# Scan stage of a ViT tower: a three-part bf16 split moved from VectorE to TensorE and ScalarE, and new instruction orders

## The reference, cut to what matters

```python
xm   = silu(conv4(xn @ W_in.T)[..., :256]); z = (xn @ W_in.T)[..., 256:]
Bt   = xm @ W_B.T          # 16 numbers per token
Ct   = xm @ W_C.T          # 16 numbers per token
dt   = softplus(xm @ W_dt.T + b_dt)            # 256 per token
dA   = exp(-exp(log_A)[None, None] * dt[..., None])
dBx  = dt[..., None] * Bt[:, :, None, :] * xm[..., None]
h    = scan over tokens of h = dA * h + dBx    # 256 x 16 states
y    = (h * Ct[:, :, None, :]).sum(-1)
out  = residual + (y * silu(z)) @ W_out.T
```

## Time and profile before

| | |
|---|---|
| median of 3 runs | 2949.59 us (2949.24 to 2952.46) |
| the profiled execution's own time | 2955.88 us |
| its span in the profile | 2954.1 us |
| VectorE busy over the span | 2447.7 us, 83% |
| TensorE busy | 2455.6 us, 83% |
| GpSimd busy | 1978.0 us, 67% |
| ScalarE busy | 1511.1 us, 51% |
| granted TensorE clock, mean | 0.924 |

### The profile page before, as it was taken

How to read it: one execution, slowest core, us unless ns; L and a number is a source line. 1 busy time by engine, 2 the same in 40 slices (tenths; PEclk the granted TensorE clock), 3 DMA queues, 4 the chain that set the end, 5 groups by cost and what they waited for, 6 DMA issues and landing times. The chain is left out here.

```text
span 2954.1 us, 25221 instructions
## 1 busy us (share of the span) xinstructions
PE 2455.6 (83%) x6718; PEld 1146.3 (39%) x6718; DVE 2447.7 (83%) x3527; ACT 1511.1 (51%) x2542; POOL 1978.0 (67%) x1008
## 2 busy tenths in 40 slices
PE   6899898898998898988973068438999999998998
PEld 2344444444444444444431033213444444444443
DVE  4999999999999999999997822137888888888875
ACT  5666666666666666676652134234444433443332
POOL 3888888888888887888882068755555555555540
PEclk9999999999999999999996579758999999999999
DMA  2333323323333323324231024310000000000000
GB/s 83 110 94 98 109 92 105 106 87 117 94 99 107 100 91 108 103 87 119 89 102 51 0 50 71 36 51 22 29 29 29 29 29 29 29 29 29 26 22 11
DMA packets 169758, 199.27 MB, mean 67 GB/s; under 512 B 38969, under 2 KB 156946, under 8 KB 169490
## 3 DMA queue, kind: packets, MB, share of 16 engines
q1 hardware_dynamic: 158354, 189.27, 20.9%
q0 software_dynamic: 11264, 8.40, 2.2%
HBM read 164.37 MB, written 33.25 MB: 67 GB/s over the span
## 5 line engine op out<-in xcount | busy, mean ns | idle before, releaser
L905 POOL TENSOR_TENSOR a_hc<-a_h,a_cs 128x896 f32<-128x896 f32 (+1 forms) x448 | 891.6, 2002 | 182.1 <-DVE a_h L744 181.2
L360 PE MATMUL a_y_bank<-a_hc,a_ident 128*128 128x448 f32 (+1 forms) x1792 | 766.7, 562 | 14.7 <-POOL a_hc L905 13.6
L537 ACT ACTIVATE a_da<-a_dt,a_neg_a 128x448 f32<-128x448 f32 (+1 forms) x896 | 548.4, 632 | 331.3 <-DVE a_h L744 330.3
L744 DVE TENSOR_TENSOR_SCAN a_h<-a_da,a_h,a_dbx 128x448 f32<-128x448 f32 x528 | 583.1, 1134 | 14.2 <-ACT a_da L537 11.9
L360 PEld LDWEIGHTS a_y_bank<-a_hc,a_ident 128*128 128x128 f32 x1792 | 344.1, 196 | 359.9 <-issue 287.2
L2086 POOL TENSOR_TENSOR c_prod<-c_prob,c_qkv 128x1024 f32<-128x1024 f32 x100 | 280.7, 2849 | 274.6 <-DVE c_prob L1973 274.6
L1670 PE MATMUL c_p_ACC<-c_sc,c_w_ex 128*128 128x512 f32 x800 | 365.4, 594 | 0.0
L2079 POOL TENSOR_TENSOR c_prod<-c_qkv 128x1024 f32<-128x1024 f32 x100 | 231.9, 2341 | 152.7 <-ACT c_qkv L1754 152.7
L728 DVE TENSOR_TENSOR a_dbx<-a_dtx,a_b_bank 128x896 f32<-128x896 f32 (+1 forms) x308 | 328.5, 1067 | 4.5 <-PE a_b_bank L353 0.7
L1947 DVE TENSOR_TENSOR c_sc<-c_hid,c_p_CB 128x1024 f32<-128x1024 f32 x200 | 239.9, 1214 | 69.6 <-PE c_p_CB L1662 67.1
L893 POOL TENSOR_TENSOR a_dbp<-a_dtx,a_bs 128x896 f32<-128x896 f32 (+1 forms) x140 | 269.7, 1936 | 0.3
(11 more groups left out here) (297 smaller groups left out, 3688.3 us busy)
## 6 DMA issues: line engine op xcount, KB each, us to landing
a_cs<-c_rows SPq DMA_DIRECT2D x96, 896.0 KB, 5.3
a_bs<-c_rows SPq DMA_DIRECT2D x24, 1120.0 KB, 5.7
a_cs<-c_rows SPq DMA_DIRECT2D x16, 900.0 KB, 4.4
c_x<-h_rows SPq DMA_DIRECT2D x25, 256.0 KB, 2.8
heads<-c_ot SPq DMA_DIRECT2D x25, 256.0 KB, 2.3
c_dealt<-heads SPq DMA_DIRECT2D x200, 32.0 KB, 1.9
rolled<-c_res SPq DMA_DIRECT2D x25, 256.0 KB, 2.1
h_rows<-a_th SPq DMA_DIRECT2D x24, 224.0 KB
```

The lines of the kernel that those rows point to most:

```text
L360: pe.matmul(y_bank[:, d, 0:g.w], ident[:], hc[:, (g.i * NS + n) % HC_RING, d, 0:g.w], start=(n == 0), stop=(n == NS - 1)).then_inc(s_sum, 1)
L537: act.activation(da[:, k % DA_RING, 0:g.w], dt[g.slot][:, d, 0:g.w], ACT.Exp, scale=neg_a[:, d * NS + n:d * NS + n + 1]).then_inc(s_da, 1)
L744: dve.tensor_tensor_scan(h[:, n, d, 0:g.w], da[:, (g.i * 2 * NS + k) % DA_RING, 0:g.w], x, state, ALU.mult, ALU.add).then_inc(s_scan, 1)
L905: pool.tensor_tensor(hc[:, (q.i * NS + n) % HC_RING, :, 0:q.w], h[:, n, :, 0:q.w], cs[:, n % C_RING, 0:q.w].unsqueeze(1).to_broadcast([P, ...
```

## The change

B's split: ScalarE rounds the PSUM tile to bf16 as before. Then TensorE subtracts that rounded part from the PSUM tile itself: a bf16 matmul with a matrix `less` (minus the identity in the columns 64 to 127, zero elsewhere) accumulates into the bank that still holds the result. ScalarE copies the remainder as bf16 (partitions 64 to 127), a second such matmul subtracts it for partitions 96 to 127, and ScalarE copies the rest. The bank is given back after this last copy. `split_b` and `low_b` on VectorE are gone. `one_more` is now an Identity activation with bias 1 on ScalarE. VectorE makes the two `less` matrices at the start. `WORK_ORDER` moves the transposed output (`trh`) to bank 0 and `logit` to bank 1. The lists of calls of PE, ACT, DVE and POOL are written in a new order; SP's list is as before.

```diff
-              ("dt1", 0, 1), ("out", 0, -1), ("trh", 1, -1), ("cen2", 0, -1), ("var2", 1, -1), ("tok", 1, 2),
-              ("logit", 0, -1), ("cen", 0, 2), ("var", 1, 2), ("trn", 1, -1))
+              ("dt1", 0, 1), ("out", 0, -1), ("trh", 0, -1), ("cen2", 0, -1), ("var2", 1, -1), ("tok", 1, 2),
+              ("logit", 1, -1), ("cen", 0, 2), ("var", 1, 2), ("trn", 1, -1))
...
+            def less_high():
+                if p:
+                    pe.wait_ge(s_bch, p.i + 1)
+                    pe.matmul(tile_of("bc", p)[:, 0:p.w], less[:, 0, :], bc[p.slot][:, 0:p.w], start=False, stop=True,
+                              skip_group_check=True).then_inc(s_less, 1)
+
+            def less_middle():
+                if p:
+                    pe.wait_ge(s_bcm, p.i + 1)
+                    pe.matmul(tile_of("bc", p)[:, 0:p.w], less[:, 1, :], bc[p.slot][:, 0:p.w], start=False, stop=True,
+                              skip_group_check=True).then_inc(s_less, 1)
...
             def middle_b():
                 if p:
-                    taken(act, "bc", p)
-                    act.copy(bc[p.slot][64:128, 0:p.w], bcr[64:128, 0:p.w]).then_inc(s_bcm, 1)
+                    act.wait_ge(s_less, 2 * p.i + 1)
+                    act.copy(bc[p.slot][64:128, 0:p.w], tile_of("bc", p)[64:128, 0:p.w]).then_inc(s_bcm, 1)
+
+            def low_b():
+                if p:
+                    act.wait_ge(s_less, 2 * p.i + 2)
+                    act.copy(bc[p.slot][96:128, 0:p.w], tile_of("bc", p)[96:128, 0:p.w]
+                             ).then_inc(s_free[nth["bc", p.i][0]], 1)
+
+            def one_more():
+                if p:
+                    act.wait_ge(s_spe, p.i + 1)
+                    need(act, s_spm, p.i)
+                    act.activation(yt[:, :, 0:p.w], spe[:, :, 0:p.w], ACT.Identity, bias=1.0).then_inc(s_spu, 1)
...
+        dve.tensor_scalar(less[:, 0, 64:P], ident[:, 64:P], -1.0, None, ALU.mult)
+        dve.tensor_scalar(less[:, 1, 96:P], ident[:, 96:P], -1.0, None, ALU.mult)
+        dve.memset(less[:, 0, 0:64], 0.0)
+        dve.memset(less[:, 1, 0:96], 0.0)
...
-            def split_b():
-                if p:
-                    w = p.w
-                    dve.wait_ge(s_bch, p.i + 1)
-                    dve.tensor_tensor(bcr[64:128, 0:w], tile_of("bc", p)[64:128, 0:w], bc[p.slot][64:128, 0:w],
-                                      ALU.subtract).then_inc(s_free[nth["bc", p.i][0]], 1)
-
-            def low_b():
-                if p:
-                    w = p.w
-                    dve.wait_ge(s_bcm, p.i + 1)
-                    dve.tensor_tensor(bc[p.slot][96:128, 0:w], bcr[96:128, 0:w], bc[p.slot][96:128, 0:w],
-                                      ALU.subtract).then_inc(s_bc, 1)
-
-            def one_more():
-                if p:
-                    w = p.w
-                    dve.wait_ge(s_spe, p.i + 1)
-                    need(dve, s_spm, p.i)
-                    dve.tensor_scalar(yt[:, :, 0:w], spe[:, :, 0:w], 1.0, None, ALU.add).then_inc(s_spu, 1)
```

More of the change, by code:

```diff
@@ L1 @@
 from contextlib import ExitStack
+from dataclasses import dataclass
 import numpy as np
@@ L479, in tensor @@
             taps(0, 0)
+            taps(0, 1)
+            b_row(2)
+            taps(1, 0)
             last_sum(14)
             last_sum(15)
-            b_row(2)
-            taps(0, 1)
-            taps(1, 0)
             b_row(4)
+            taps(1, 1)
             sum_state(0)
-            taps(1, 1)
-            sum_state(1)
-            b_row(5)
             gate(0)
             gate(1)
+            b_row(5)
+            step(0)
             b_row(7)
-            step(0)
+            sum_state(1)
             b_and_c()
             b_row(8)
+            step(1)
             sum_state(2)
-            step(1)
+            out()
             sum_state(3)
-            out()
             b_row(10)
+            turn_out()
             sum_state(4)
             b_row(11)
+            less_high()
             sum_state(5)
-            turn_out()
             center_out()
+            less_middle()
+            sum_state(6)
+            variance_out()
+            sum_state(7)
             b_row(13)
-            sum_state(6)
-            sum_state(7)
-            variance_out()
+            token()
             sum_state(8)
-            token()
+            b_row(14)
             logit()
+            center()
             sum_state(9)
+            variance()
+            next_b_row()
             sum_state(10)
-            b_row(14)
-            center()
-            variance()
             sum_state(11)
+            turn_norm()
             sum_state(12)
-            turn_norm()
-            next_b_row()
             sum_state(13)
@@ L678, in scalar @@
             decays(5)
+            decays(6)
             biased(0)
-            decays(6)
-            keep_b_and_c()
             decays(7)
             biased(1)
-            middle_b()
+            decays(8)
             small_exp()
-            decays(8)
+            keep_b_and_c()
+            one_more()
             decays(9)
             keep_rows()
+            middle_b()
+            decays(10)
             square_out()
+            low_b()
+            decays(11)
+            log_of_sum()
             tail()
-            log_of_sum()
-            decays(10)
-            decays(11)
             scale_out()
@@ L835, in vector @@
             scans(1, 0)
+            product(2)
             scans(1, 1)
-            product(2)
-            gated()
             scans(2, 0)
@@ L841, in vector @@
             scans(3, 0)
+            gated()
             scans(3, 1)
@@ L846, in vector @@
             scans(4, 1)
+            scans(5, 0)
             product(7)
-            scans(5, 0)
             scans(5, 1)
@@ L851, in vector @@
             scans(6, 1)
-            split_b()
+            scans(7, 0)
             product(8)
-            scans(7, 0)
             scans(7, 1)
@@ L857, in vector @@
             scans(8, 0)
+            scans(8, 1)
             product(10)
-            scans(8, 1)
             scans(9, 0)
+            scans(9, 1)
             product(11)
[L862 to L865, removed]
             scans(10, 0)
@@ L868, in vector @@
             scans(11, 0)
-            normed_out()
+            lost()
             scans(11, 1)
             product(13)
+            normed_out()
             scans(12, 0)
             scans(12, 1)
-            steps()
             scans(13, 0)
@@ L878, in vector @@
             scans(14, 0)
+            scans(14, 1)
+            steps()
             normed()
             normed_twice()
-            scans(14, 1)
             scans(15, 0)
+            scans(15, 1)
             next_product()
-            scans(15, 1)
     def gpsimd(pool):
@@ L938, in gpsimd @@
             weigh(0)
+            weigh(1)
             product(6)
-            weigh(1)
             weigh(2)
+            weigh(3)
             product(9)
-            product(12)
-            weigh(3)
             weigh(4)
             weigh(5)
-            product(15)
+            product(12)
             weigh(6)
             weigh(7)
+            product(15)
             weigh(8)
@@ L955, in gpsimd @@
             weigh(12)
+            weigh(13)
             stepped()
-            weigh(13)
             weigh(14)
             weigh(15)
+            kept()
             next_product(3)
-            kept()
     def after_a(eng):
```

7 lines of the change are left out of this document (4 added, 3 removed).

## The result

| | before | changed |
|---|---|---|
| median | 2951.03 us (2949.24 to 2956.58) | 2850.47 us (2848.34 to 2854.72) |
| profiled execution, own time | 2955.88 us | 2854.72 us |
| span | 2954.1 us | 2852.9 us |

The ratio of changed to before is 0.9662, 95% interval 0.9647 to 0.9676. On a second chip, beside three experiments, it was 0.9639 (0.9611 to 0.9667). Forecast were 2851 us and a range of 2834 to 2892.

The account below looks back on a forecast made before the run. VectorE, busy 97.5% of the scan stage's steady part, was taken as the bound; 27 turns at 3.79 us less gave -102.3, the start +3.6, together -98.7 us: 2851 us, range 2834 to 2892.

Parts of the forecast that it names:

- Per turn: Scan-stage turn: 3.56 us off VectorE plus 0.43 for `normed`, less 0.20 possibly uncovered, gives 3.79 us less; turn 50.2 us.
- The whole: Whole kernel: 102.3 us gained over 27 turns, 3.6 us lost at the start, 98.7 us less in sum.
- `low_b`'s wait "is removed like work": On VectorE: some 1.6 of `low_b`'s 2.24 us is a wait for GpSimd, claimed to go with the instruction.
- `normed`'s 0.43 us: VectorE's idle time before `normed`, waiting for ScalarE's `scales`, 0.43 us a turn, counted as gone in the new order.
- What is added is hidden: TensorE's added 0.4 us a turn and ScalarE's rise from 35.8 to 37.3 us fit beside VectorE's turn of about 50.
- The ring's cover: Product 10, `b_row(11)`, `less_high`, middle copy, state 10's decays: 1.9 us against 3.3 us of VectorE work, cover 1.4 us.
- `b_row(5)` behind the gates: TensorE's later spread makes VectorE wait some 0.4 us for product 5, within the wait for the silus; 0.1 us charged.
- Rival 2: Port wait moves to `steps`, up to 1.6 us longer beside a GpSimd product: 43 us, time 2894; chance 0.08.
- Rival 1: Small stalls, TensorE late at spreads or ring short of cover: 0.5 to 1.5 us a turn, time 2878; chance 0.20.
- rival 4: The 0.52 us wait for the silus goes as well: 14 us more gain, time 2837; chance 0.09.
- Start: Before the first scan: 0.6 us for making `less`, 3.0 us for the token matmul's later bank, together 3.6 us more.
- The sign "the later stages move by more than 3 us": Stages behind the scan stage were forecast untouched; moving by more than 3 us would show the prediction wrong.

Follow-up runs that it names:

- e1: Kernel before, in its old orders, with `low_b` removed and the third part of B left out of the result: 2937.81 us, ratio to before 0.9933.
- e3: Kernel before with the split work and `one_more` moved to TensorE and ScalarE, in before's orders and banks: 2917.67 us, ratio to before 0.9863.
- e2: Changed kernel's new orders and banks, with `split_b`, `one_more` and `low_b` still on VectorE and no `less` matmuls: 2915.87 us, ratio to before 0.9865.
- e10: Moved work in before's orders, with `one_more` on ScalarE placed behind the decays of state 8 instead of ahead: 2872.40 us, ratio to before 0.9715.
- e9: Changed kernel with `less_high` one sum (1.50 us) later on TensorE, behind `sum_state(5)`: 2870.38 us, ratio to before 0.9718.
- e7: Changed kernel with `less_high` 3.75 us later on TensorE, behind `sum_state(6)`, `less_middle` right behind it: 2939.68 us, ratio to before 0.9949.
- e4: Changed kernel with `b_row(5)` between the two gates on TensorE and product 7 ahead of state 5's scans on VectorE: 2839.51 us, ratio to before 0.9604.
- e6: Changed kernel with `steps` one scan earlier on VectorE, ahead of the second scan of state 14: 2882.47 us, ratio to before 0.9752.
- e8: Filled kernel without `lost` on VectorE, `one_more` writing zeros, the softplus correction left out of the result: 2809.87 us, ratio to before 0.9519.
- filled kernel: Changed kernel with `b_row(5)` between the gates and product 7 ahead of state 5's scans; two runs: 2839.51 and 2840.38 us, ratios 0.9604 and 0.9617.

## Why the prediction was right, point by point

- **Per turn**: 3.79 us forecast, 3.98 measured, nearly the 3.56 + 0.43 without the 0.20 charged for what might stay uncovered. The turn itself was forecast at 50.2 us and is 50.51: the 53.96 us it was taken from had the short first distance in it, and was 54.49.
- **The whole**: 98.7 us less forecast, 101.2 measured between the two spans. That it came so near is in part luck. The products from first to last gained 105.2 us (102.3 forecast), the start cost 4.9 (3.6), the end of the stage 3.1 (not in the sum), and the stages behind gave 4.0 (0 forecast).
- **`low_b`'s wait "is removed like work"**: right for the change, wrong for `low_b` by itself. e1 shows that the wait doesn't belong to `low_b`: taken out alone in the old order it moves to `lost`, 20 us instead of 61. The 1.6 us a turn go in either of two ways. With `one_more` and `low_b` both off VectorE, `lost` starts 0.17 us ahead of GpSimd's product, in the old orders too (e3, 1.07 us). And in the new orders GpSimd has nothing to run while VectorE reaches `lost`; e2 shows it with `low_b` still there (0.62 us). The change does both, so the sum came out.
- **`normed`'s 0.43 us**: gone, as forecast.
- **What is added is hidden**: only with ScalarE's work placed anew. Alone the moved work brings 1.41 us a turn of its 3.56 (e3), for VectorE's removed instructions had also covered ScalarE's long stretches. The prediction checked that cover for the new list alone. One instruction moved in ScalarE's list brings it to 3.22 (e10).
- **Interaction**: orders alone 1.61 us a turn, work alone 1.41, both 3.98, which is 0.96 more than the sum. Two things of opposite sign lie in it. The 1.6 us of the wait for GpSimd are in each half's gain, but only once in the whole. And the waits for ScalarE that the moved work makes in the old orders, 1.4 us in each turn and near 1.75 in 13 of 24, by an estimate from these figures 2.3 us on average, are gone in the new ones.
- **The ring's cover**: 1.4 us worked out. In the trace the first decay of state 10 is done at 692.46 and its scan starts at 693.74, 1.28 us. e9 and e7 both give 1.25.
- **`b_row(5)` behind the gates**: forecast 0.4 us, hidden within the wait for the silus. Measured 0.41, with 0.19 left behind it. Right; rival 4's gain lay there too, and e4 took it.
- **Rival 2**: a port wait on `steps` as a remainder. It occurs: most executions take 1.06 us, but there are ones of 1.33 and 1.86, on average 0.06 us a turn. e6 gives the full price, 1.32 us a turn.
- **Rival 1**: TensorE busy for 94% and not the bound, and e8 shows that there was room for one us more. The sum of the issue times was the better guide than its busy share.
- **Start**: 3.6 us forecast, 4.9 measured at the first product. On the second chip the changed kernel has its first product at 52.3 us, so 1.4 of the 4.9 differ from one execution to the next. From TensorE's last `step` matmuls (35.16 us before, 35.98, on the second chip 34.65) to the first product it is 4.0 us more in both executions, for which 3.0 were forecast. The token's matmul makes 0.84 of the difference: it took 1.86 us at a granted clock of 0.50, where the forecast had the 1.02 of the earlier trace rows.
- **The end of the stage**: 3.1 us longer, and not in the sum. `trh` now shares a bank with the matmul behind it, and `logit` with the transposes behind it. In the last turn, which has nothing else to run, TensorE waits 0.77 us for the copy of the one and 0.70 for the copy of the other, which it didn't before, and the logits take 1.66 instead of 0.91 us, at a granted clock of 0.51 instead of 0.94.
- **The sign "the later stages move by more than 3 us"**: they moved by 4.0. The filled kernel's two runs, the same program, differ by 9.1 us in the same part (1367.5 and 1376.6 us from the first instruction behind the scan stage to the end), so this sign was set too fine to decide anything.

## What to carry to other kernels

When an instruction is long because it waits, ask what stands behind it: the wait stays in the program until either the instruction that causes it or the meeting itself is moved. An instruction on the bounding engine may be the cover for another engine's long stretch; taking it away and placing the loaded engine's work anew are one change. The orders alone brought two fifths of the gain, the moved work alone one third, the moved work with one instruction placed anew four fifths. Work added to an engine with spare time must be cut between the pieces that the bounding engine waits for.

## What the runs showed of the hardware beyond that

TensorE's clock made one short wait cost twice: after a wait of 2.4 to 2.6 us it fell to 0.50 for the next matmuls in 13 of 24 turns and stayed at 1.00 in 11 (e3), after one of 1.59 us it stayed (e10), and VectorE's second wait of 1.75 us came and went with it. In the kernel before, GpSimd's products with C took up to 2.70 us; in the changed one, where `steps` no longer starts just ahead of one, the longest of 448 takes 1.99 us:

```profile
L915 POOL TENSOR_TENSOR a_hc<-a_h,a_cs x448: 1911/1937/1987, 58.0 to 1464.9; 128x896 f32<-128x896 f32 x128, 128x900 f32<-128x900 f32 x22
```
